# The opening of a four-image attention kernel on one core: x in four pieces, projections reordered, and the first weights' low parts made by GpSimd

## The chip, the core and the metric

The kernel runs on one core of a Trainium2 chip. The metric is the device time of one execution in microseconds (us), median of three runs. TensorE is the matmul engine (PE in the rows, PEld its weight loads), VectorE is DVE, ScalarE is ACT, GpSimd is POOL; SyncE (SP) only issues DMAs here. The engines run their instruction lists in order and wait for each other by semaphores.

## The reference

For each of four images `x` of 256 channels by 1024 pixels:

```python
q = einsum('oc,bcn->bon', Wq, xf) + bq        # 32 x 1024
k = einsum('oc,bcn->bon', Wk, xf) + bk        # 32 x 1024
v = einsum('oc,bcn->bon', Wv, xf) + bv        # 256 x 1024
scores = einsum('bqi,bqj->bij', q, k)         # 1024 x 1024
attn = softmax(scores, axis=-1)
out = einsum('bcj,bij->bci', v, attn) + x
```

## The kernel before

Every fp32 operand of a matmul is split in two: a high part, rounded to the matmul's type by a copy (a *cut*), and a low part, the difference (a *split*, a subtraction). A product is then high by high, low by high and high by low. A cut is a copy on ScalarE, VectorE or GpSimd; a split is a subtraction on VectorE or GpSimd.

Channels lie on partitions in two tiles (`CT` = 2). The work on one image has these stages:

- Projection of q and k (`qk_home`), q and k biased, cut, split and stacked into `q_a` and `k_a`, so that one matmul of 96 rows gives all three products. For image 0 `q_a` is filled in parts `Q_PARTS`: two quarters and the second half (called q2, cut and split by GpSimd in `split_q2`).
- Scores of pixel tile t (128 pixels by 1024) in PSUM, `first_scores(t)` for image 0. VectorE takes the negated maximum per row (`row_max`), ScalarE the sum of exponentials (`sum_exp`), which together are the shift of the softmax. VectorE turns the shifts into rows of `q_b`.
- v, projected in eight tiles (`v_tile`), two to a half bank, cut (`first_cut_v`) and split (`split_v`).
- Transposed scores (`scores_t(n)`, 128 by 512) with the shift in the matmul, exponentials by ScalarE (`exp(n)`: `w_full`, and for some n also the high part `w_hi`), the low part `w_lo` by VectorE or GpSimd (`split_w(n)`), and the weighting (`weigh_v`): four matmuls with `w_hi` and two with `w_lo`, the low products. There are 16 such tiles n per image.

Which engine makes `w_lo` of tile n is a table, `split_by_pool(n)`. In the steady state a table `FRONT` puts the projection and scores of the next image between the weighting steps of this one. Everything before the first weighting is written out by hand on each engine and is the opening; the first weighting step, `first_weigh_v`, is the last of it.

In the opening SyncE loads x of image 0 as two transfers of 512 KB, one for each channel tile, and then `wv`; ScalarE issues the transfer of `small_sb` (the weights of q and k, and the biases). ScalarE cuts x in four pieces of 512 columns, `piece(i)`; VectorE makes their low parts; TensorE runs three matmuls for each piece. Until then TensorE multiplies zeros (`keep_busy`). GpSimd copies `wqk_pair` (used from image 1 on), splits `wv`, copies the q quarters to their second place (`put_q_dup`), does `split_q2`, and then cuts and splits image 1's x in four quarters (`cut_x1`, `split_x1`), with `split_w(1)` and `split_w(3)` behind them. `shift_ready` stands for VectorE's shifts of the first four tiles; GpSimd's third quarter waits for it. `v_split` counts VectorE's splits of v.

Of the kernel before, what the change touches and what calls it, by code (L numbers as in the profile page):

```python
# [6 lines left out]
def nonlocal_attention(nc, x, small, wv_t, out):  # L7
# [6 lines left out]
    P = 128  # L14
# [24 lines left out]
    def split_by_pool(n):  # L39
        return n % PER in ((1, 3, 8, 9, 11, 13) if n < PER else (0, 8, 9, 11, 13))  # L40
# [19 lines left out]
    with ctx:  # L60
# [51 lines left out]
        x0_in = [sem(f"x0_in{c}") for c in range(CT)]  # L112
# [80 lines left out]
        def piece(i):  # L193

            return i // 2, cols(i % 2)
# [80 lines left out]
        def _(sp):  # L276
            for c in range(CT):
                sp.dma_start(x_sb[:, 0, c, :], x_v[0, :, c, :]).then_inc(x0_in[c], DMA)
# [82 lines left out]
        def _(pool):  # L361
# [52 lines left out]


# [6 lines left out]
            pool.wait_ge(pair_made, 2)  # L422
            pool.wait_ge(wv_cut, 1)
# [3 lines left out]
            put_q_dup(0)  # L427
            pool.wait_ge(q_dup_put, 1)
            put_q_dup(1)
            pool.wait_ge(q_dup_put, 2)  # L430
# [12 lines left out]
            pool.wait_ge(x1_split, 3)  # L443
            cut_x1(3)
            pool.wait_ge(x1_cut, 4)

            split_w(1)
# [36 lines left out]
        def _(act):  # L484
            act.dma_start(small_sb[:, :], small).then_inc(small_in, DMA)
            act.preload_act_table_set("natural_log_exp_and_others")
            for i in range(4):
                c, part = piece(i)
                act.wait_ge(x0_in[c], DMA)
                nc.scalar.activation(x_hi[:, 0, c, part], x_sb[:, 0, c, part], ACT.Copy).then_inc(x0_cut, 1)  # L490
# [66 lines left out]
            def put_q_hi():  # L557

                act.wait_ge(q_lo_put, 1)
                nc.scalar.activation(q_a[2 * CQK:3 * CQK, Q_PARTS[1]], q_home(1),  # L560
                                     ACT.Identity, bias=bias[2 * CQK:3 * CQK, 0:1]).then_inc(q_hi_put, 1)
# [17 lines left out]
            exp(0)  # L579
# [33 lines left out]
        def _(dve):  # L613
# [5 lines left out]
            def twice(w):  # L619
# [5 lines left out]
            dve.wait_ge(wqk_cut, 1)  # L625
            nc.vector.tensor_tensor(twice(wqk_lo), wqk, twice(wqk_hi).bitcast(fp32),
                                    ALU.subtract).then_inc(wqk_split, 1)

            for i in range(4):
                c, part = piece(i)  # L630
                dve.wait_ge(x0_cut, i + 1)
# [119 lines left out]
            def finish(b, h, c):  # L751
# [9 lines left out]
                if (b, h) == (0, 0):  # L761
# [84 lines left out]
        def _(pe):  # L846
# [23 lines left out]
            def first_project_qk(i):  # L870
                c, part = piece(i)
                dst = qk_home(0, i % 2)
                if i == 0:
                    pe.wait_ge(wqk_cut, 1)
                pe.wait_ge(x0_cut, i + 1)
                nc.tensor.matmul(dst, wqk_hi[:, c, :], x_hi[:, 0, c, part], start=(c == 0), stop=False)
                if i == 0:
                    pe.wait_ge(wqk_split, 1)
                nc.tensor.matmul(dst, wqk_lo[:, c, :], x_hi[:, 0, c, part], start=False, stop=False)
                pe.wait_ge(x0_split, i + 1)  # L880
                last = nc.tensor.matmul(dst, wqk_hi[:, c, :], x_lo[:, 0, c, part], start=False, stop=(c == CT - 1))  # L881
                if c == CT - 1:
                    last.then_inc(qk_ready, 1)
# [55 lines left out]
            def v_tile(b, t):  # L939
# [4 lines left out]
                if b == 0 and t == 0:  # L944

                    for c in range(CT):
                        for xs in (x_hi, x_lo):
                            nc.tensor.matmul(dst, xs[:, 0, c, px], wv_hi[:, c, :],
                                             start=(c == 0 and xs is x_hi), stop=False)
                    pe.wait_ge(wv_split, 1)  # L950
                    for c in range(CT):
                        nc.tensor.matmul(dst, x_hi[:, 0, c, px], wv_lo[:, c, :], start=False, stop=(c == CT - 1))
                    return
                last = group(dst, terms)
                if t % VT == VT - 1:
                    last.then_inc(v_ready, 1)

# [75 lines left out]
            def first_weigh_v():  # L1033
# [57 lines left out]
            v_tile(0, 3)  # L1091
            first_scores(3)
# [10 lines left out]
            def turn(b):  # L1103
                for s in range(PER):
# [15 lines left out]
                    if what == S:  # L1120
                        if b + image:
                            scores(b + image, k)
                        else:
# [40 lines left out]
```

## Time and profile before

| what | us |
|---|---|
| median of three runs | 164.04 (163.82 to 164.06) |
| the profiled execution | 163.81 |
| its span in the trace | 162.0 |
| TensorE busy | 157.5 |
| VectorE busy | 133.9 |
| ScalarE busy | 109.2 |
| GpSimd busy | 60.0 |

The span is what the trace covers, from the first instruction of the program to the last; the execution's own time has 1.8 us around it. A busy share is an average over stages: the opening, some 19 us, has other limits than the rest. In timeline rows the first number is the start in us from the span's beginning and the second the time busy; with "x4" the row merges four instructions and the time is that from the first's start to the last's end.

### The profile page before, as it was taken

Reading aid. Unit: us, or ns where it says so; the run is one execution under the profiler, and the core shown is the slowest. Engines: PE = TensorE matmul, PEld = TensorE weight load, DVE = VectorE, ACT = ScalarE, POOL = GpSimd, SP = SyncE. Lnnn points to the kernel's source line nnn. Section 1 sums busy time; section 2 is a strip of 40 time slices with the busy share of each in tenths; the row PEclk is TensorE's granted clock in tenths of the full one; section 3 lists DMA queues with packets and bytes.
Section 4 is the critical chain, followed back from the end, with each engine's and each line's share of the span. In section 5 each row is a group of like instructions: output and inputs, shape, how many; then the busy total and the mean of one; then the engine's idle time right before and its main releaser. Section 6 shows DMA issues by size and latency. Waiting matters only on the chain.

```text
span 162.0 us, 2456 instructions
## 1 busy us (share of the span) xinstructions
PE 157.5 (97%) x788; PEld 132.3 (82%) x788; DVE 133.9 (83%) x215; ACT 109.2 (67%) x200; POOL 60.0 (37%) x68
## 2 busy tenths in 40 slices
PE   7999999999999999999999999999999999999993
PEld 5677887798888887798888897788888898888882
DVE  1899998888988989997989989895989779846952
ACT  3679887969999545827999646736896655756400
POOL 4479946256222316348443300342333300124500
PEclk9999999999999999999999999999999999999999
DMA  4576672152103030162711130162320330003003
GB/s 161 187 299 166 243 235 89 31 151 63 55 0 97 1 129 2 37 144 67 268 39 49 54 129 0 37 146 67 121 61 1 97 129 0 0 5 129 0 0 130
DMA packets 7780, 14.67 MB, mean 91 GB/s; under 512 B 1504, under 2 KB 2072, under 8 KB 7768
## 3 DMA queue, kind: packets, MB, share of 16 engines
q1 hardware_dynamic: 6728, 13.46, 25.4%
q0 software_dynamic: 608, 0.80, 2.2%
q10 hardware_dynamic: 432, 0.26, 0.5%
q8 instruction: 6, 0.10, 0.3%
q14 instruction: 6, 0.05, 0.1%
HBM read 4.79 MB, written 4.20 MB: 55 GB/s over the span
## 4 chain that ended last, share of the span: by engine, by line
PE 90%; DMA 2%; ACT 2%; DVE 2%; issue 1%; DVEq 0%
PE acc L1009 32%; PE acc L1015 16%; PE slot L849 11%; PE st L996 9%; PE slot L909 7%; PE slot L1009 5%; DMA small_sb<-small 2%; PE slot L1015 2%; ACT dump L504 2%; PE slot L861 2%; PE slot L866 2%; PE slot L935 1%; DVE negmax L667 1%; PE slot L881 1%; DVE x_lo L632 0%
## 5 line engine op out<-in xcount | busy, mean ns | idle before, releaser
L402 POOL TENSOR_TENSOR w_lo<-w_full,w_hi 128x512 fp32r<-128x512 f32 x21 | 28.0, 1338 | 46.6 <-ACT w_full L542 25.4
L1009 PE MATMUL acc<-w_hi,v_hi 128*128 128x512 f32 x112 | 44.3, 395 | 0.0
L1009 PE MATMUL acc<-w_hi,v_lo 128*128 128x512 f32 x112 | 44.1, 394 | 0.0
L542 ACT ACTIVATE w_full<-st 128x512 f32<-128x512 f32 x62 | 36.8, 594 | 7.6 <-PE st L996 7.5
L504 ACT ACTIVATE dump<-slot,negmax 128x1024 f32<-128x1024 f32 x29 | 32.5, 1119 | 10.5 <-DVE negmax L667 10.1
L667 DVE TENSOR_REDUCE negmax<-slot 128x1 f32<-128x1024 f32 x29 | 35.2, 1217 | 2.7 <-PE slot L909 2.7
L1015 PE MATMUL acc<-w_lo,v_hi 128*128 128x512 f32 x112 | 37.4, 396 | 0.0
L734 DVE TENSOR_TENSOR w_lo<-w_full,w_hi 128x512 fp32r<-128x512 f32 x43 | 30.7, 719 | 3.6 <-issue 0.5
L1009 PEld LDWEIGHTS acc<-w_hi,v_hi 128*128 128x128 f32 x112 | 21.1, 189 | 5.0 <-issue 0.2
L1009 PEld LDWEIGHTS acc<-w_hi,v_lo 128*128 128x128 f32 x112 | 21.2, 189 | 4.8
L1015 PEld LDWEIGHTS acc<-w_lo,v_hi 128*128 128x128 f32 x112 | 21.0, 188 | 4.8
L996 PE MATMUL st<-q_b,k_b 98*128 98x512 f32 x62 | 24.5, 398 | 0.1
L725 DVE CAST w_hi<-w_full 128x512 fp32r<-128x512 f32 x40 | 19.5, 489 | 3.0 <-ACT w_full L542 1.5
L539 ACT ACTIVATE w_hi<-st 128x512 fp32r<-128x512 f32 x24 | 14.3, 594 | 6.2 <-PE st L996 6.0
L849 PE MATMUL slot<-wv_hi,x_hi 128*128 128x256 f32 x62 | 17.4, 281 | 0.4 <-ACT dump L504 0.4
L849 PE MATMUL slot<-wv_lo,x_hi 128*128 128x256 f32 x62 | 17.4, 281 | 0.0
L849 PE MATMUL slot<-wv_hi,x_lo 128*128 128x256 f32 x62 | 17.3, 280 | 0.0
L909 PE MATMUL slot<-k_a,q_a 96*128 96x512 f32 x48 | 15.2, 397 | 0.0
L531 ACT ACTIVATE v_hi<-slot 128x512 fp32r<-128x512 f32 x12 | 7.2, 599 | 11.8 <-PE slot L849 11.8
L265 POOL DMA_DIRECT2D q_b<-shift_rows x7 | 4.2, 602 | 29.5 <-DVE shift_rows L706 27.0
L715 DVE TENSOR_TENSOR v_lo<-slot,v_hi 128x512 fp32r<-128x512 f32 x16 | 11.0, 690 | 3.8 <-ACT v_hi L531 3.7
L909 PEld LDWEIGHTS slot<-k_a,q_a 96*128 96x128 f32 x48 | 13.0, 310 | 1.1
(102 smaller groups left out, 225.2 us busy)
## 6 DMA issues: line engine op xcount, KB each, us to landing
out<-x_sb SPq DMA_DIRECT2D x7, 512.0 KB, 2.8
x_sb<-x SPq DMA_DIRECT2D x3, 1024.0 KB, 5.1
k_b<-k_a SPq DMA_DIRECT2D x8, 192.0 KB, 2.6
q_b<-q_a SPq DMA_DIRECT2D x8, 192.0 KB, 2.6
x_sb<-x SPq DMA_DIRECT2D x2, 512.0 KB, 4.2
k_a<-qk_parts SPq DMA_DIRECT2D x12, 64.0 KB, 2.0
q_a<-qk_parts SPq DMA_DIRECT2D x12, 64.0 KB, 2.2
k_a<-qk_parts POOLq DMA_DIRECT2D x6, 64.0 KB, 2.2
```

The lines of the kernel that those rows point to most:

```text
L402: nc.gpsimd.tensor_tensor(w_lo[:, r, :], w_full[:, r, :], w_hi[:, r, :].bitcast(fp32), ALU.subtract).then_inc(w_split_pool, 1)
L504: nc.scalar.activation(dump[:, t % 2, :], s_home(b, t), ACT.Exp, bias=negmax[:, t:t + 1], accum_out=rowsum[:, t:t + 1]).then_inc(rowsum_re ...
L539: nc.scalar.activation(w_hi[:, r, :], st_home(n), ACT.Exp).then_inc(w_cut_act, 1)
L542: nc.scalar.activation(w_full[:, r, :], st_home(n), ACT.Exp).then_inc(exp_done, 1)
L667: nc.vector.tensor_reduce(out=negmax[:, t:t + 1], in_=s_home(b, t), op=ALU.max, axis=AX.X, negate=True).then_inc(negmax_ready, 1)
L725: nc.vector.tensor_copy(w_hi[:, r, :], w_full[:, r, :]).then_inc(w_cut_dve, 1)
L734: nc.vector.tensor_tensor(w_lo[:, r, :], w_full[:, r, :], w_hi[:, r, :].bitcast(fp32), ALU.subtract).then_inc(w_split_dve, 1)
L849: last = nc.tensor.matmul(dst, lhs, rhs, start=(i == 0), stop=(i == len(terms) - 1))
L909: last = nc.tensor.matmul(s_home(b, t)[:, cols(h)], pixels(b, t), k_a[0:K_A, cols(h)], start=True, stop=True)
L996: nc.tensor.matmul(st_home(n), k_b[0:K_B, j * P:(j + 1) * P], q_b[0:K_B, cols(h)], start=True, stop=True).then_inc(st_ready, 1)
L1009: nc.tensor.matmul(dst, v[:, b % 2, j, c * P:(c + 1) * P], w_hi[:, n % RING, part], start=(j == 0 and v is v_hi), stop=False)
L1015: return nc.tensor.matmul(dst, v_hi[:, b % 2, j, c * P:(c + 1) * P], w_lo[:, n % RING, part], start=False, stop=(j == JT - 1))
```

## The change

The table gives tile 0's low part to GpSimd, which makes it just before that of tile 1 and ahead of its cut of x1's last quarter. On TensorE the low products of tile 0 come behind the scores of tile 5, the sixth tile, and not behind those of tile 4. Besides:

- x of image 0 comes in four transfers of 256 KB, each with its semaphore, in the order of the halves (both channel tiles of the first 512 pixels, then the second). The small transfer is issued by SyncE behind the first.
- The projection of q and k is ordered by halves, so the first half is through before the second.
- ScalarE makes the high part of q's first quarter (VectorE did) and cuts `wv` only behind the high parts of q and k. Its first cut of v stands behind the sums.
- GpSimd copies q's first quarter ahead of `wqk_pair` and the second behind it, then splits `wv`.
- TensorE's high products for v tile 0 stand behind tile 0's scores, its low ones and v tile 1 behind the scores of tile 2; tile 3's scores stand before v tile 3.
- VectorE splits k before q, and v's second pair of tiles before the first.

```diff
-        return n % PER in ((1, 3, 8, 9, 11, 13) if n < PER else (0, 8, 9, 11, 13))
+        return n % PER in ((0, 1, 3, 8, 9, 11, 13) if n < PER else (0, 8, 9, 11, 13))
...
-            return i // 2, cols(i % 2)
+            return i % CT, cols(i // CT)
...
-            for c in range(CT):
-                sp.dma_start(x_sb[:, 0, c, :], x_v[0, :, c, :]).then_inc(x0_in[c], DMA)
+            for i in range(4):
+                c, part = piece(i)
+                sp.dma_start(x_sb[:, 0, c, part], x_v[0, :, c, part]).then_inc(x0_in[i], DMA)
+                if i == 0:
+                    sp.dma_start(small_sb[:, :], small).then_inc(small_in, DMA)
...
+            put_q_dup(0)
+            pool.wait_ge(q_dup_put, 1)
...
             pool.wait_ge(pair_made, 2)
+            put_q_dup(1)
+            pool.wait_ge(q_dup_put, 2)
             pool.wait_ge(wv_cut, 1)
...
-            put_q_dup(0)
-            pool.wait_ge(q_dup_put, 1)
-            put_q_dup(1)
-            pool.wait_ge(q_dup_put, 2)
...
             pool.wait_ge(x1_split, 3)
+            split_w(0)
+            split_w(1)
             cut_x1(3)
             pool.wait_ge(x1_cut, 4)
 
-            split_w(1)
...
-            act.dma_start(small_sb[:, :], small).then_inc(small_in, DMA)
...
+            act.wait_ge(small_in, DMA)
+            put_k_hi(0)
+            put_q_hi(0)
+            put_k_hi(1)
+            put_q_hi(1)
             act.wait_ge(wv_in, DMA)
             nc.scalar.activation(wv_hi[:, :, :], wv[:, :, :], ACT.Copy).then_inc(wv_cut, 1)
-            act.wait_ge(small_in, DMA)
-            put_k_hi(0)
-            put_k_hi(1)
-            put_q_hi()
             put_q2_full()
-            first_cut_v(0)
             for t in range(TH):
                 sum_exp(0, t)
             put_first_rows()
+            first_cut_v(0)
...
-            dve.wait_ge(qk_ready, 1)
-            nc.vector.tensor_scalar(out=q_a[2 * CQK:3 * CQK, Q_PARTS[0]], in0=q_home(0),
-                                    scalar1=bias[2 * CQK:3 * CQK, 0:1], scalar2=None,
-                                    op0=ALU.add).then_inc(q_hi_put, 1)
+            put_k_lo(0)
             put_q_lo(0)
-            put_k_lo(0)
...
             first_shifts()
-            split_v(0, 0)
             first_cut_v(1)
             split_v(0, 1)
+            first_cut_v(2)
+            split_v(0, 0)
             invert_sums()
-            first_cut_v(2)
             split_v(0, 2)
...
                 if h == 0 and j % VT == 0:
-                    pe.wait_ge(v_split, 4 * b + 1 + j // VT)
+
+                    pe.wait_ge(v_split, 4 * b + 1 + j // VT if b + j else 2)
...
                 first_scores(TH)
+                scores_t(AHEAD)
+
+                first_scores(TH + 1)
                 for c in range(CT):
                     last = weigh_low(0, 0, 0, c, acc[:, c, :], slice(0, HALF))
                 last.then_inc(av_done, 1)
-                scores_t(AHEAD)
...
-            keep_busy(20, QUARTER)
-            for i in range(4):
-                first_project_qk(i)
-            pe.wait_ge(wv_cut, 1)
-            v_tile(0, 0)
-            v_tile(0, 1)
+            keep_busy(16, QUARTER)
+            first_project_all()
+
+            keep_busy(4, QUARTER)
             first_scores(0)
+            first_v_high()
             first_scores(1)
             first_scores(2)
+            first_v_low()
+            v_tile(0, 1)
 
             pe.wait_ge(q2_full_put, 1)
             v_tile(0, 2)
+            first_scores(3)
             v_tile(0, 3)
-            first_scores(3)
```

On GpSimd, from the copy of the weight pair to q2, this stood before:

```order
L418 CAST wqk_pair<-wqk_hi 128x2x64 [waits wqk_cut,ones_put]
L418 CAST wqk_pair<-wqk_lo 128x2x64 [waits wqk_split]
L424 TENSOR_TENSOR wv_lo<-wv,wv_hi 128x512 [waits wv_cut,pair_made]
L374 CAST q_a<-q_a 32x256 [waits q_hi_put,wv_split]
L374 CAST q_a<-q_a 32x256 [waits q_hi_put,q_dup_put]
L380 CAST q_a<-qk_rest 32x512 [waits q2_full_put,q_dup_put]
```

and now:

```order
L377 CAST q_a<-q_a 32x256 [waits q_hi_put,ones_put]
L423 CAST wqk_pair<-wqk_hi 128x2x64 [waits wqk_cut,q_dup_put]
L423 CAST wqk_pair<-wqk_lo 128x2x64 [waits wqk_split]
L377 CAST q_a<-q_a 32x256 [waits q_hi_put,pair_made]
L431 TENSOR_TENSOR wv_lo<-wv,wv_hi 128x512 [waits wv_cut,q_dup_put]
L383 CAST q_a<-qk_rest 32x512 [waits q2_full_put,wv_split]
```

The two copies of q have moved ahead of the split of `wv`, one of them ahead of the pair; `wv_lo` is now the last before q2.

On GpSimd, from the third quarter of image 1's x on, before:

```order
L408 CAST x_hi<-x_sb 128x2x256 [waits shift_ready,x1_split]
L412 TENSOR_TENSOR x_lo<-x_sb,x_hi 128x2x256 [waits x1_cut]
L408 CAST x_hi<-x_sb 128x2x256 [waits x1_split]
L402 TENSOR_TENSOR w_lo<-w_full,w_hi 128x512 [waits w_cut_act,exp_done,x1_cut]
L402 TENSOR_TENSOR w_lo<-w_full,w_hi 128x512 [waits w_cut_act,exp_done,w_split_dve]
```

and now:

```order
L411 CAST x_hi<-x_sb 128x2x256 [waits shift_ready,x1_split]
L415 TENSOR_TENSOR x_lo<-x_sb,x_hi 128x2x256 [waits x1_cut]
L405 TENSOR_TENSOR w_lo<-w_full,w_hi 128x512 [waits w_cut_act,exp_done,x1_split]
L405 TENSOR_TENSOR w_lo<-w_full,w_hi 128x512 [waits w_cut_act,exp_done]
L411 CAST x_hi<-x_sb 128x2x256
```

The low parts of weights 0 and 1 stand directly behind the third quarter, and the cut of the last quarter behind both.

On TensorE, at the end of the opening (`acc<-w_hi` is the weighting with high weights, `acc<-w_lo` the low products, `slot<-k_a` scores, `st<-q_b` transposed scores), before:

```order
L1009 MATMUL acc<-w_hi,v_lo 128x512
L935 MATMUL slot1<-k_a,q_a 128x512 [waits v_split,q2_lo_put,q2_dup_put]
L935 MATMUL slot1<-k_a,q_a 128x512
L1015 MATMUL acc<-w_lo,v_hi 128x512 [waits w_split_dve] x2
L996 MATMUL st<-q_b,k_b 128x512 [waits exp_done]
L935 MATMUL slot0<-k_a,q_a 128x512 [waits v_split]
L935 MATMUL slot0<-k_a,q_a 128x512
```

and now:

```order
L1026 MATMUL acc<-w_hi,v_lo 128x512
L948 MATMUL slot1<-k_a,q_a 128x512 [waits v_split,q2_lo_put,q2_dup_put]
L948 MATMUL slot1<-k_a,q_a 128x512
L1012 MATMUL st<-q_b,k_b 128x512 [waits exp_done]
L948 MATMUL slot0<-k_a,q_a 128x512 [waits v_split]
L948 MATMUL slot0<-k_a,q_a 128x512
L1032 MATMUL acc<-w_lo,v_hi 128x512 [waits w_split_pool] x2
```

The low products have moved behind three matmuls, and wait for GpSimd instead of VectorE.

## Rows read from the trace of the kernel before

**Rows 1.** The page's chain that ended last: shares of the span by engine.

```profile
PE 90%; DMA 2%; ACT 2%; DVE 2%; issue 1%; DVEq 0%
```

**Rows 2.** Busy time by stretch: length, PE, PEld, DVE, ACT, POOL, clock, DMA, GB/s.

```profile
4.50:5.00 0.50, 0.50 (x4) 0.38 (x3) 0.29 (x1) 0.50 (x1) 0.00 (x0) 1.00 0.97 401
...
40.00:80.00 40.00, 40.00 (x197) 33.95 (x197) 36.44 (x58) 29.29 (x55) 16.27 (x16) 1.00 0.26 79
```

**Rows 3.** The chain in order of time: start, us, what.

```profile
0.75 3.94 DMA small_sb<-small
...
18.42 0.71 PE slot L849 x6
```

**Rows 4.** DMAs: x's time from issue to landing, and the small weights'.

```profile
DMA to landing us min/median/max: 3.7/4.6/4.8
...
small_sb<-small ACTq DMA_DIRECT2D x1, 66.0 KB, 3.9
```

**Rows 5.** Timeline of the projection: start, us, engine, line, operation.

```profile
4.50 1.15 ACT L490 ACTIVATE x_hi<-x_sb 128x512 fp32r<-128x512 f32 x2 [2.04 <-DMA x_sb<-x]
...
5.04 0.43 DVE L626 TENSOR_TENSOR wqk_lo<-small_sb,wqk_hi 128x256 fp32r<-128x256 f32 x1
...
5.27 0.59 PE L876 MATMUL slot<-x_hi,wqk_hi 128*128 128x512 f32 x1
5.38 2.68 DVE L632 TENSOR_TENSOR x_lo<-x_sb,x_hi 128x512 fp32r<-128x512 f32 x4
...
5.70 0.40 PE L879 MATMUL slot<-x_hi,wqk_lo 128*128 128x512 f32 x1
...
8.41 0.39 PE L881 MATMUL slot<-x_lo,wqk_hi 128*128 128x512 f32 x1
```

**Rows 6.** Timeline behind it: wv, k and q, and the first maximum.

```profile
6.88 0.62 ACT L569 ACTIVATE wv_hi<-wv 128x512 fp32r<-128x512 f32 x1
...
8.21 1.31 ACT L554 ACTIVATE k_a<-slot,small_sb 64x512 fp32r<-64x512 f32 x2 [0.72 <-PE slot L881]
...
9.18 1.40 DVE L642 SCALAR_TENSOR_TENSOR k_a<-slot,small_sb,k_a 32x512 fp32r<-32x512 f32 x2
...
9.55 0.47 ACT L560 ACTIVATE q_a<-slot,small_sb 32x256 fp32r<-32x256 f32 x1
...
11.17 1.23 DVE L667 TENSOR_REDUCE negmax<-acc 128x1 f32<-128x1024 f32 x1
```

**Rows 7.** Timeline of GpSimd, VectorE's split of weights 0, and GpSimd's w_lo (ns).

```profile
5.14 0.47 POOL L418 CAST wqk_pair<-wqk_hi 128x128 fp32r<-128x128 f32 x1 [2.30 <-DVE wqk_hi L624]
...
5.56 0.75 POOL L418 CAST wqk_pair<-wqk_lo 128x128 fp32r<-128x128 f32 x1
...
7.64 1.58 POOL L424 TENSOR_TENSOR wv_lo<-wv,wv_hi 128x512 fp32r<-128x512 f32 x1 [1.34 <-ACT wv_hi L569]
...
10.72 0.61 POOL L380 CAST q_a<-qk_rest 32x512 fp32r<-32x512 f32 x1 [0.18 <-ACT qk_rest L565]
...
19.53 0.68 DVE L734 TENSOR_TENSOR w_lo<-w_full,w_hi 128x512 fp32r<-128x512 f32 x1
19.59 1.10 POOL L408 CAST x_hi<-x_sb 128x512 fp32r<-128x512 f32 x1
...
L402 POOL TENSOR_TENSOR w_lo<-w_full,w_hi x21: 1283/1297/1721, 20.9 to 152.4; 128x512 fp32r<-128x512 f32 x21
```

**Rows 8.** Timeline of TensorE at the first weighting steps.

```profile
18.97 0.47 PE L1009 MATMUL acc<-w_hi,v_hi 128*128 128x512 f32 x1
...
21.63 0.39 PE L996 MATMUL st<-q_b,k_b 98*128 98x512 f32 x1
...
23.25 0.84 PE L935 MATMUL slot<-k_a,q_a 96*128 96x512 f32 x2
...
23.93 0.39 PE L996 MATMUL st<-q_b,k_b 98*128 98x512 f32 x1
```

**Rows 9.** The page's costliest groups: VectorE's split of v, mean ns.

```profile
L715 DVE TENSOR_TENSOR v_lo<-slot,v_hi 128x512 fp32r<-128x512 f32 x16 | 11.0, 690 | 3.8 <-ACT v_hi L531 3.7
```

More of the change, by code:

```diff
@@ L110, in nonlocal_attention @@
         slot = [ctx.enter_context(nc.psum_tensor(f"slot{i}", [P, N], fp32)) for i in range(2)]
-        x0_in = [sem(f"x0_in{c}") for c in range(CT)]
+        x0_in = [sem(f"x0_in{i}") for i in range(4)]
         x1_in = sem("x1_in")
@@ L488, in _ @@
                 c, part = piece(i)
-                act.wait_ge(x0_in[c], DMA)
+                act.wait_ge(x0_in[i], DMA)
                 nc.scalar.activation(x_hi[:, 0, c, part], x_sb[:, 0, c, part], ACT.Copy).then_inc(x0_cut, 1)
@@ L555, in put_k_hi, with put_q_hi @@
                                      ACT.Identity, bias=bias[0:2 * CQK, 0:1]).then_inc(k_hi_put, 1)
-            def put_q_hi():
-                act.wait_ge(q_lo_put, 1)
-                nc.scalar.activation(q_a[2 * CQK:3 * CQK, Q_PARTS[1]], q_home(1),
+            def put_q_hi(i):
+                if i:
+                    act.wait_ge(q_lo_put, i)
+                nc.scalar.activation(q_a[2 * CQK:3 * CQK, Q_PARTS[i]], q_home(i),
                                      ACT.Identity, bias=bias[2 * CQK:3 * CQK, 0:1]).then_inc(q_hi_put, 1)
@@ L624, in _ @@
             nc.vector.tensor_copy(twice(wqk_hi), wqk).then_inc(wqk_cut, 1)
-            dve.wait_ge(wqk_cut, 1)
-            nc.vector.tensor_tensor(twice(wqk_lo), wqk, twice(wqk_hi).bitcast(fp32),
-                                    ALU.subtract).then_inc(wqk_split, 1)
             for i in range(4):
                 c, part = piece(i)
+                if i == 1:
+                    dve.wait_ge(wqk_cut, 1)
+                    nc.vector.tensor_tensor(twice(wqk_lo), wqk, twice(wqk_hi).bitcast(fp32),
+                                            ALU.subtract).then_inc(wqk_split, 1)
                 dve.wait_ge(x0_cut, i + 1)
@@ L868, in project_qk, with first_project_qk, first_project_all @@
                 both_halves(CT - 1).then_inc(qk_ready, 1)
-            def first_project_qk(i):
+            def first_project_qk(i, w, xs):
                 c, part = piece(i)
[L872 to L883, printed above, removed]
+                return nc.tensor.matmul(qk_home(0, i // CT), w[:, c, :], xs[:, 0, c, part],
+                                        start=(c == 0 and w is wqk_hi and xs is x_hi),
+                                        stop=(c == CT - 1 and xs is x_lo))
+            def first_project_all():
+                pe.wait_ge(wqk_cut, 1)
+                pe.wait_ge(x0_cut, 1)
+                first_project_qk(0, wqk_hi, x_hi)
+                pe.wait_ge(x0_split, 1)
+                first_project_qk(0, wqk_hi, x_lo)
+                pe.wait_ge(x0_cut, 2)
+                first_project_qk(1, wqk_hi, x_hi)
+                pe.wait_ge(wqk_split, 1)
+                first_project_qk(0, wqk_lo, x_hi)
+                first_project_qk(1, wqk_lo, x_hi)
+                pe.wait_ge(x0_split, 2)
+                first_project_qk(1, wqk_hi, x_lo).then_inc(qk_ready, 1)
+                for i in (2, 3):
+                    pe.wait_ge(x0_cut, i + 1)
+                    first_project_qk(i, wqk_hi, x_hi)
+                    first_project_qk(i, wqk_lo, x_hi)
+                    pe.wait_ge(x0_split, i + 1)
+                    last = first_project_qk(i, wqk_hi, x_lo)
+                last.then_inc(qk_ready, 1)
             def pixels(b, t):
@@ L943, in v_tile @@
                          for xs, w in ((x_hi, wv_hi), (x_hi, wv_lo), (x_lo, wv_hi))]
[L944 to L953, printed above, removed]
                 last = group(dst, terms)
@@ L956, in v_tile, with first_v_high, first_v_low @@
                     last.then_inc(v_ready, 1)
+            def first_v_high():
+                pe.wait_ge(wv_cut, 1)
+                for c in range(CT):
+                    for xs in (x_hi, x_lo):
+                        nc.tensor.matmul(v_home(0, 0)[:, 0:C], xs[:, 0, c, 0:P], wv_hi[:, c, :],
+                                         start=(c == 0 and xs is x_hi), stop=False)
+            def first_v_low():
+                pe.wait_ge(wv_split, 1)
+                for c in range(CT):
+                    nc.tensor.matmul(v_home(0, 0)[:, 0:C], x_hi[:, 0, c, 0:P], wv_lo[:, c, :],
+                                     start=False, stop=(c == CT - 1))
             def project_v(b, g):
@@ L1122, in turn @@
                             scores(b + image, k)
-                        else:
+                        elif s:
                             first_scores(k)
```

## The prediction

> **What bounds the kernel now.** I read the chain of waits first. It lies on TensorE for 90% of the span, and its largest lines are the products with v [rows 1]. Then I read the busy time by stretch: from 40 to 80 us TensorE is busy 40.00 us of 40 [rows 2]. From the first weighting at 18.97 us on, matmuls follow each other at 0.23 us per 512 columns, with one hole that counts: the scores of tile 6, at 23.25, take 0.84 us for two, and the next matmul is at 23.93 where 23.25 + 0.46 would be 23.71: 0.22 late [rows 8]. The change leaves TensorE's later work alone, so only the opening can move the time. The question is when TensorE is through the low products of the first weights and whether it runs without a hole from there. In the opening the chain starts with a DMA, 3.94 us for the small weights [rows 3].
>
> **Landings.** The two 512 KB halves of x land 3.7 and about 4.6 us after their issues at 0.74 and 1.2, so at 4.45 and 5.8; the small weights at 4.66 [rows 4]. At 401 GB/s [rows 2] 256 KB take 0.65 us. With pieces of 256 KB I estimate the first at 4.45 - 0.65 = 3.8, the small weights behind it at 4.0 (66 KB, 0.17 us), the next pieces at 4.65, 5.3 and 5.95. No row shows a first piece of this size; bounds are 3.45 (another 256 KB less in flight in the slow beginning) and 4.3 (as slow as the whole half, nearly). I take 3.8.
>
> **Projection of q and k.** ScalarE cuts piece 0 in 0.61 us, to 4.45. VectorE then does four x_lo (2.68 us) and wqk_lo (0.36 from start to start) from 4.5 to 7.55; the second x_lo ends at 6.25 [rows 5]. The matmul behind it ends near 6.7, where the first half had been ready at 8.11; the last of twelve starts at 7.7 and ends at 8.1, against 8.80 [rows 5]. From here by the rows' durations [rows 6]: ScalarE k_hi(0) 6.8 to 7.5, q_hi(0) to 7.95, k_hi(1) 8.2 to 8.9, VectorE k_lo(0) 7.55 to 8.3, q_lo(0) to 8.8, then ScalarE q_hi(1) 8.85 to 9.3, wv_hi 9.25 to 9.85, q2_full to 10.5; VectorE k_lo(1) 8.95 to 9.7, q_lo(1) to 10.15. The first maximum starts at 10.2 instead of 11.17: 0.97 us earlier.
>
> **TensorE until the first weights.** Behind tile 0's scores come four matmuls, the scores of 1 and 2, the low products of v (wv_lo at 11.25, below), and two v tiles of 0.71 each [rows 3], so tile 3's scores are through at 13.7, where VectorE, three maxima of 1.13 behind 10.2, would be free at 13.6: 0.1 of the 0.97 is lost there. The fourth maximum, the shifts, the sum, the rows and v tiles 6 and 7 are the same operations in the same order as before and keep 0.87. VectorE has to give two splits of v before the weighting may start (one before), and the order cut, split, cut, split at 0.7 each [rows 9] behind the shifts (before near 16.3, then 15.4) has them at 18.1 to 18.2, the same. The weighting starts at 18.1 instead of 18.97 [rows 8].
>
> **GpSimd.** Here the gain goes. The copy of q (0) waits for q_hi(0), 8.0 to 8.4. The two copies of the weight pair stand behind it now. They took 0.47 and 0.75 beside VectorE's subtractions; alone I take 0.32 each, to 9.1 (bounds: 0.61 for four times the elements in the same kind of copy says it could be 0.2, the two rows say 0.47 and 0.75). Copy (1) 9.35 to 9.75. wv_lo waits for wv_hi, 9.9, and ran 1.58 us while VectorE's x_lo reached 0.42 us into it, to 8.06 [rows 5, 7]; the same form on w_lo takes 1.297 median, 1.283 to 1.721 [rows 7]. I take 1.29, to 11.25, for VectorE then has only work from PSUM. q2 starts at 11.3, before 10.72 [rows 7]. From q2's first copy to the end of the third x_lo of image 1 the order is unchanged: 19.59 - 10.72 = 8.87 us without a gap over 0.2 [rows 7]. So the subtraction of weights 0, which VectorE did at 19.53 [rows 7], starts at 20.2, ends at 21.5, and TensorE can use it at 21.55.
>
> TensorE comes to those low products at 18.1 + 0.93 (four high) + 0.47 (scores 4) + 0.23 (transposed 2) + 0.47 (scores 5) = 20.2. It stands for 1.35 us. Queued behind the waiting matmul are transposed scores 3, the weighting with tile 1 and all that follows, and ScalarE's exponentials wait for these. The two low products end at 22.0. Before, the same set of work was done at 21.63, where transposed scores 3 start [rows 8]: 0.39 us late. Weights 1 follow on GpSimd at once, 21.5 to 22.8; TensorE wants them at 22.0 + 0.23 + 0.93 = 23.2, in time. Scores 6 then start at 23.65, their sum condition long met, so the hole of 0.22 goes. Sum: +0.39 - 0.22 = **+0.17 us**.
>
> What costs nothing: the copy of a quarter of x1 put behind the weights would be due 3 us later. VectorE loses 0.6 us of subtraction and gains a slack that nobody waits for. The four extra idle matmuls (16 + 4 in place of 20) fill 0.47 us of the wait for k_lo. The last transposed scores, issues on SP and DMAs of k_b and q_b come earlier or have over 3 us.
>
> A row on the common path: the copy of x1's last quarter took 1.10 us at 19.59, where its three sisters took 0.61, and VectorE was subtracting w_lo from 19.53 to 20.21 [rows 7]. The Trainium skill (SBUF — State Buffer, Who interferes with whom) says that a VectorE instruction with two SBUF inputs and a GpSimd one that reads SBUF lock each other out, the second waiting until the first is through; the trace agrees. By that rule VectorE's two small shift operations near 15.2 would also wait for GpSimd's x_lo, up to 0.7 us, and VectorE's cut of weights 2, near 22.1, until 22.8. In my sum neither counts: the weighting would start at 18.8 rather than 18.1, inside the 1.35 us of standing, and weights 2 are wanted at 24.1. By the rule the sum would stay +0.17.
>
> **The profiled execution** took 163.81, so 163.98 after; the median of the three runs is 0.23 above it, which gives 164.2 for the measured time.
>
> **Rivals.**
> *GpSimd is in time or nearly (faster).* If pieces land at the early bound and hand-offs cost less than in my steps, q2 starts at 10.7, as it did before, weights 0 are ready at 20.95 and the two low products end at 21.4: 0.23 ahead, with the hole another 0.22, 0.45 in all: 163.6. For it: 3.45 is not excluded. Against it: 0.6 us must be found in six hand-offs that the rows price. If GpSimd did not bind at all, 1.35 more than the forecast could be won, 162.9, which I hold for out of reach.
> *GpSimd's chain is longer (slower).* It decides from the point where q2 starts after 11.45. wv_lo at 1.58 again adds 0.29, the pair copies at 0.47 and 0.75 push copy (1) and add 0.1, a first landing at 4.1 adds 0.2: +0.6 and so 164.8. For it: all three prices stand in rows.
> *TensorE runs the projection at half rate (slower).* The first two real matmuls start 0.43 us apart (5.27 to 5.70) [rows 5], later ones 0.23. Those 0.43 for 512 columns are the 1.2 GHz level, although the granted clock reads 1.00 there [rows 2]. In the changed order it has holes around 5, at 8.5 and of 0.7 us before k_lo(1). If the rise comes only after the projection, eleven matmuls cost 0.20 more each, 2.2 us, of which 0.3 lie in waits for x_lo: q and k are ready near 10.0, 1.9 later, and all of it goes through GpSimd's chain: 166.1. The Trainium skill (TensorE: Matmul & The Clock Gate, What's actually happening) says that activity releases the clock and idleness takes it back, which speaks for this rival; that the clock rose within the projection in this trace speaks against it.
> *The change does not do what it says*: the first piece lands at 4.45 as the whole half did. Then GpSimd's chain is 0.65 longer, 164.9; I count this with the second rival.
>
> **Chances.** Forecast (own range 163.8 to 164.6) 0.62; GpSimd in time 0.14; longer chain 0.16; half rate 0.08. A measurement of this kernel can tell about 0.2%, 0.33 us, from no change. Of the forecast's 0.62 some 0.04 lies below 163.71 and 0.16 above 164.37. So faster 0.18, same 0.42, slower 0.40. The range goes down just past the faster rival, to 163.5, and up past the longer chain, to 165.0; the half-rate case is left out.
>
> **What would show it.** Right: q and k's first half ready near 6.7, the first maximum near 10.2, the weighting from 18.1 to 18.8, GpSimd without a gap from wv_lo at 9.9 to the end of weights 1, and a hole of about a microsecond before TensorE's first low products, put down to GpSimd's w_lo; from 24 us on TensorE as before, some 0.2 later. Wrong: if that hole is under 0.5 us, if GpSimd's w_lo starts before 19.6, if matmuls after 5.3 stand 0.43 apart, or if TensorE shows holes behind 24 us.

## The result, and the profile after

| | before | after |
|---|---|---|
| median, us | 163.96 (163.80 to 164.20, 6 runs) | 165.63 (165.05 to 166.06, 6 runs) |
| profiled execution, us | 163.81 | 165.60 |
| its span, us | 162.0 | 163.8 |

The ratio is 1.0099, interval 1.0075 to 1.0123: the change makes the kernel 1.67 us slower. 164.2 was forecast (163.98 for the profiled execution), and 165.0 was the top of the range.

The chain of waits of after still lies on TensorE, but a DMA of x has taken the place of the small weights' [rows 1, 3]:

```profile
PE 88%; ACT 3%; DMA 3%; POOL 1%; DVE 1%; SPq 1%; issue 0%; DVEq 0%; POOLq 0%
```

The same chain in order of time (start, us, what) leads from the third piece of x, issued at 2.12 and landed at 6.80, over q and k, the last maximum and ScalarE's sums to GpSimd's chain:

```profile
2.12 4.68 DMA x_sb<-x
7.51 1.94 PE slot L873 x6
...
15.20 1.24 DVE negmax L672
16.46 1.21 ACT dump L507 x2
20.55 1.06 POOL x_lo L415
21.69 1.29 POOL w_lo L405
```

The beginning of after's timeline (start, us, engine, line, operation) answers to rows 5:

```profile
0.74 0.38 SPq L279 DMA_DIRECT2D x_sb<-x  x1
1.19 0.42 SPq L281 DMA_DIRECT2D small_sb<-small  x1
1.65 1.38 SPq L279 DMA_DIRECT2D x_sb<-x  x3
3.07 0.43 SPq L282 DMA_DIRECT2D wv<-wv_t  x1
3.60 0.63 ACT L493 ACTIVATE x_hi<-x_sb 128x512 fp32r<-128x512 f32 x1 [1.57 <-DMA x_sb<-x]
3.78 0.29 DVE L629 CAST wqk_hi<-small_sb 128x256 fp32r<-128x256 f32 x1 [2.50 <-DMA small_sb<-small]
...
5.42 0.63 ACT L493 ACTIVATE x_hi<-x_sb 128x512 fp32r<-128x512 f32 x1 [1.18 <-DMA x_sb<-x]
...
6.82 1.23 ACT L493 ACTIVATE x_hi<-x_sb 128x512 fp32r<-128x512 f32 x2 [0.78 <-DMA x_sb<-x]
...
7.96 0.66 ACT L557 ACTIVATE k_a<-slot,small_sb 64x512 fp32r<-64x512 f32 x1
```

The first piece and the small weights land as forecast (3.6 and 3.8). The second piece lands at 5.4 instead of 4.65, the last two at 6.8 instead of 5.3 and 5.95, and ScalarE, which takes its list in order, can make k's high part only at 7.96, when it has cut both. Busy time by stretch (length, PE, PEld, DVE, ACT, POOL, clock, DMA share, GB/s) says how the queue went; first after:

```profile
3.00:4.00 1.00, 1.00 (x6) 0.69 (x5) 0.22 (x1) 0.40 (x1) 0.00 (x0) 1.00 0.79 202
4.00:5.00 1.00, 0.84 (x5) 0.33 (x2) 0.81 (x3) 0.23 (x1) 0.00 (x0) 1.00 0.81 250
5.00:6.00 1.00, 0.51 (x1) 0.19 (x1) 0.29 (x1) 0.58 (x1) 0.00 (x0) 1.00 0.89 311
```

then before, in the first two of the same stretches:

```profile
3.00:4.00 1.00, 1.00 (x6) 0.71 (x5) 0.00 (x0) 0.00 (x0) 0.00 (x0) 1.00 1.06 410
4.00:5.00 1.00, 1.00 (x7) 0.73 (x5) 0.29 (x1) 0.50 (x1) 0.00 (x0) 1.00 0.99 408
```

In these two stretches after's DMA engines are busy for 79 and 81% of the time and move 49 and 61% of the bytes. The rest of after's opening in the timeline (answers to rows 6 to 8):

```profile
11.52 1.22 DVE L672 TENSOR_REDUCE negmax<-acc 128x1 f32<-128x1024 f32 x1
...
12.80 0.60 POOL L383 CAST q_a<-qk_rest 32x512 fp32r<-32x512 f32 x1
...
16.19 1.29 POOL L415 TENSOR_TENSOR x_lo<-x_sb,x_hi 128x512 fp32r<-128x512 f32 x1
...
16.53 0.97 DVE L679 CAST shift_parts<-negmax 128x4 fp32r<-128x4 f32 x1
...
20.28 0.50 PE L1026 MATMUL acc<-w_hi,v_hi 128*128 128x512 f32 x1
...
21.69 2.52 POOL L405 TENSOR_TENSOR w_lo<-w_full,w_hi 128x512 fp32r<-128x512 f32 x2
...
23.02 0.73 PE L1032 MATMUL acc<-w_lo,v_hi 128*128 128x512 f32 x2 [0.36 <-POOL w_lo L405]
23.59 0.40 PE L1012 MATMUL st<-q_b,k_b 98*128 98x512 f32 x1
...
25.70 0.39 PE L1012 MATMUL st<-q_b,k_b 98*128 98x512 f32 x1
```

The first maximum comes at 11.52 (before 11.17), q2 on GpSimd at 12.80 (10.72), the weighting at 20.28 (18.97), transposed scores 3 at 23.59 (21.63) and 4 at 25.70 (23.93): 1.77 us late, and from there on the difference stays at that to the end. All of it is lost in the opening.

### The profile page after: what moved, and what is told of

Same layout as the page of the kernel before. It is cut to its first block, busy times and chain, and to the rows that moved or that the text cites. A ratio compares the mean times of both kernels' runs of the same rounds, so it can differ in the third digit from the quotient of the medians.

```text
span 163.8 us, 2459 instructions
## 1 busy us (share of the span) xinstructions
PE 157.5 (96%) x788; PEld 131.5 (80%) x788; DVE 134.1 (82%) x213; ACT 110.1 (67%) x201; POOL 59.7 (36%) x69
## 4 chain that ended last, share of the span: by engine, by line
PE 88%; ACT 3%; DMA 3%; POOL 1%; DVE 1%; SPq 1%; issue 0%; DVEq 0%; POOLq 0%
PE acc L1026 31%; PE acc L1032 16%; PE slot L850 11%; PE st L1012 8%; PE slot L922 7%; PE slot L1026 5%; DMA x_sb<-x 3%; PE slot L1032 2%; PE slot L862 2%; PE slot L867 2%; PE slot L873 1%; PE slot L948 1%; POOL w_lo L405 1%; DVE negmax L672 1%; ACT dump L507 1%; POOL x_lo L415 1%
## 5 line engine op out<-in xcount | busy, mean ns | idle before, releaser
L405 POOL TENSOR_TENSOR w_lo<-w_full,w_hi 128x512 fp32r<-128x512 f32 x22 | 29.3, 1334 | 46.0 <-ACT w_full L545 25.2
L739 DVE TENSOR_TENSOR w_lo<-w_full,w_hi 128x512 fp32r<-128x512 f32 x42 | 30.0, 719 | 3.3
L1026 PEld LDWEIGHTS acc<-w_hi,v_lo 128*128 128x128 f32 x112 | 21.2, 189 | 4.8
```

The costliest lines, as they stand in the source:

```text
L405: nc.gpsimd.tensor_tensor(w_lo[:, r, :], w_full[:, r, :], w_hi[:, r, :].bitcast(fp32), ALU.subtract).then_inc(w_split_pool, 1)
L739: nc.vector.tensor_tensor(w_lo[:, r, :], w_full[:, r, :], w_hi[:, r, :].bitcast(fp32), ALU.subtract).then_inc(w_split_dve, 1)
L1026: nc.tensor.matmul(dst, v[:, b % 2, j, c * P:(c + 1) * P], w_hi[:, n % RING, part], start=(j == 0 and v is v_hi), stop=False)
```

## The experiments

Each run's time is compared with runs of the kernel before on the same chip (medians 163.82 to 163.88). Two questions were put: what made the opening late, and what the named part of the change costs (weights 0 subtracted by GpSimd, the low products behind the sixth tile's scores). Trace rows are of one execution per kernel, and a number in brackets behind another is that of the kernel before.

### The small transfer back on ScalarE

```diff
                 sp.dma_start(x_sb[:, 0, c, part], x_v[0, :, c, part]).then_inc(x0_in[i], DMA)
-                if i == 0:
-                    sp.dma_start(small_sb[:, :], small).then_inc(small_in, DMA)
...
+            act.dma_start(small_sb[:, :], small).then_inc(small_in, DMA)
             act.preload_act_table_set("natural_log_exp_and_others")
```

> The changed kernel with one thing put back: the small weights' transfer is issued by ScalarE on its own queue, not by SyncE between x's first two pieces. Theory A (pieces of 256 KB in 2 KB rows on one queue move slowly by themselves, 190 to 300 GB/s where 4 KB rows moved at 400): the last pieces still land near 6.8 us, the small weights at 4.6 and not 3.75, the time stays at 165.3 to 166.0. Theory B (the small transfer's short rows inside SyncE's queue slow the pieces behind it): piece 2 lands near 4.7 instead of 5.4, the last near 6.0 instead of 6.8, and the time falls by about 0.8 us, to 164.8.

Measured: 164.69 us, ratio 1.0050 (1.0034 to 1.0067), 0.94 us less than after. Its timeline:

```profile
0.74 1.80 SPq L279 DMA_DIRECT2D x_sb<-x  x4
...
4.77 1.34 ACT L492 ACTIVATE x_hi<-x_sb 128x512 fp32r<-128x512 f32 x2 [0.36 <-DMA x_sb<-x]
...
6.38 0.63 ACT L492 ACTIVATE x_hi<-x_sb 128x512 fp32r<-128x512 f32 x1 [0.27 <-DMA x_sb<-x]
...
11.67 0.60 POOL L381 CAST q_a<-qk_rest 32x512 fp32r<-32x512 f32 x1
...
15.42 0.95 DVE L678 CAST shift_parts<-negmax 128x4 fp32r<-128x4 f32 x1
...
20.56 2.53 POOL L403 TENSOR_TENSOR w_lo<-w_full,w_hi 128x512 fp32r<-128x512 f32 x2
...
21.89 0.74 PE L1031 MATMUL acc<-w_lo,v_hi 128*128 128x512 f32 x2 [0.36 <-POOL w_lo L403]
```

The second piece is in at 4.77, the last at 6.38, and everything behind is 1.1 us earlier. The four issues on SyncE stand 0.46 us apart; with the small one among them the later pieces are issued that much later too. So the place of the 66 KB transfer costs some 0.9 us. What is left, 0.8 us over before, has another cause. The third piece shows the cost best: its cut started at 6.82 in after and 6.94 in after_no_gps (below), which has the same transfers; in small_by_act it is done by 6.11. The second piece varies by itself: it was cut at 5.42 in after, but at 4.73 in after_no_gps.

### Two transfers, four transfers, two queues

*two_transfers*: after with the small one on ScalarE and x in two transfers of 512 KB.

```diff
-            for i in range(4):
-                c, part = piece(i)
-                sp.dma_start(x_sb[:, 0, c, part], x_v[0, :, c, part]).then_inc(x0_in[i], DMA)
+            for c in range(CT):
+                sp.dma_start(x_sb[:, 0, c, :], x_v[0, :, c, :]).then_inc(x0_in[c], DMA)
...
```

> The changed kernel with x in two transfers of 512 KB as before and the small weights issued by ScalarE; the order of all arithmetic stays changed. Theory A and B both put x's halves at 4.45 and 5.8 us again. The projection by halves is then through for the first half near 7.6 (changed: 7.9) and for the second near 9.0 (changed: 9.4), so 0.4 us earlier than in the changed kernel: 165.2. Theory C (the transfers do not matter, the order of the work behind them does): no change, 165.6.

Measured: 165.30 us, ratio 1.0119 (1.0082 to 1.0157); the interval is wide, since two of its six runs were near 167. The first maximum is at 11.22, q2 at 12.50: 0.3 us earlier than in after, as is the time.

*before_four*: the reverse edit in the kernel before, whose piece order (by channel tiles) stays.

> The kernel before with one thing changed: x comes in four transfers of 256 KB on SyncE's queue, in the old order (both halves of channel tile 0, then of tile 1), the small weights still on ScalarE's queue. Theory A: the last piece lands 0.8 to 1.0 us later than the second half did (6.7 instead of 5.8), and the time rises to about 164.8. Theory B: it lands at 5.8 or 5.9 and the time stays at 164.0.

Measured: 163.81 us, ratio 0.9995 (0.9980 to 1.0010), single runs from 163.24 to 164.53. Four pieces in one queue cost nothing here, as theory B had it, but gain nothing either. The first maximum is at 10.71 (11.17), and q2 at 10.11 (10.72). In the profiled execution (164.35, one of the longer of its twelve) the gain is lost at the shifts, where two rows of its timeline stand over each other:

```profile
15.54 1.27 POOL L413 TENSOR_TENSOR x_lo<-x_sb,x_hi 128x512 fp32r<-128x512 f32 x1
...
15.64 1.18 DVE L677 TENSOR_TENSOR shift_parts<-negmax,shift_parts 128x4 fp32r<-128x4 f32 x1
```

An operation on 4 elements per partition, 0.17 us where it is alone, ends when GpSimd's subtraction does. This wait of one engine for the other is called the lock below.

*two_queues*: after with the named part undone, the small transfer and pieces 1 and 3 issued by ScalarE.

> As the kernel with both things put back (small weights on ScalarE's queue, VectorE subtracting for weights 0), with x's pieces 1 and 3 issued by ScalarE behind the small weights and pieces 0 and 2 by SyncE. Theory H (what limits the pieces is the one queue that carries them): the pieces land 0.3 to 0.6 us sooner, the last at 5.7, and the time is 163.6. Theory I (the total rate near 400 GB/s limits them): the last at 6.2 to 6.4 as on one queue, ScalarE's issues of 0.4 us each cost nothing before 3.6 us, and the time is that of the kernel on one queue.

Measured: 165.18 us, ratio 1.0093 (1.0066 to 1.0121). The first maximum is at 10.86, later than with one queue in the kernel that it is to be compared with (small_by_act_no_gps, below: 10.65 and 165.03). The second queue bought nothing here.

### The named part alone, and taken away

*headline_on_before*: the kernel before with only the named part.

```diff
-        return n % PER in ((1, 3, 8, 9, 11, 13) if n < PER else (0, 8, 9, 11, 13))
+        return n % PER in ((0, 1, 3, 8, 9, 11, 13) if n < PER else (0, 8, 9, 11, 13))
...
+            split_w(0)
+            split_w(1)
             cut_x1(3)
...
                 first_scores(TH)
+                scores_t(AHEAD)
+                first_scores(TH + 1)
                 for c in range(CT):
                     last = weigh_low(0, 0, 0, c, acc[:, c, :], slice(0, HALF))
                 last.then_inc(av_done, 1)
-                scores_t(AHEAD)
...
-                        else:
+                        elif s:
                             first_scores(k)
```

The last lines keep the sixth tile's scores, now issued in the opening, from being issued a second time.

> The kernel before with the named part of the change alone: GpSimd subtracts for weights 0 and 1 ahead of its cut of x1's last quarter, and TensorE's low products of weights 0 stand behind the scores of the sixth tile. Theory D (GpSimd's subtraction is what the time is lost on): GpSimd's queue is at this point at 19.59, gives weights 0 at 20.9, and TensorE arrives at 21.1, so even here it has no slack; if anything is late, a hole of some tenths and 164.2. Theory E (the loss comes from the opening before it; here the subtraction is in time): no hole, VectorE is free 0.6 us earlier and takes the fifth tile's maximum at 20.6, and the hole of 0.22 us before tile 6's scores goes: 163.75.

Measured: 164.40 us, ratio 1.0029 (1.0018 to 1.0040): slower. But not in the opening: the low products start at 21.37, 0.14 behind the matmul before them, and transposed scores 4 start at 23.95 (23.93). The loss is at 42 us, on VectorE:

```profile
42.31 0.69 DVE L735 TENSOR_TENSOR w_lo<-w_full,w_hi 128x512 fp32r<-128x512 f32 x1 [0.50 <-issue]
42.92 1.22 DVE L668 TENSOR_REDUCE negmax<-slot 128x1 f32<-128x1024 f32 x1
44.05 1.56 DVE L638 TENSOR_TENSOR x_lo<-x_sb,x_hi 128x512 fp32r<-128x512 f32 x1
```

VectorE stands for 0.50 us for nothing that the profile shows ("issue"). That puts its subtraction behind GpSimd's `w_lo` of 43.77, which it then has to sit out (1.56 instead of 0.68); from 52 us on TensorE is 0.67 later. The kernel before has one such stall as well, elsewhere. Its `w_lo` there is followed at once by the next operation (102.47):

```profile
101.75 0.69 DVE L734 TENSOR_TENSOR w_lo<-w_full,w_hi 128x512 fp32r<-128x512 f32 x1 [0.46 <-issue]
```

*gps_with_filler*: the same kernel with an instruction put on VectorE where the moved subtraction had stood, so that its list keeps its length.

```diff
+            nc.vector.memset(filler[:, :], 0.0)
             split_v(0, 3)
...
```

> The named part of the change alone on the kernel before, as in the run that took 164.40, with one addition: a memset of 128 by 8 on VectorE, whose result nobody reads, where its subtraction for weights 0 stood, so that its list has as many instructions as before. In the 164.40 run the two traces agreed within 0.02 us until 42 us; there VectorE stood 0.50 us before a subtraction for no wait that the profile shows (in the kernel before such a stand of 0.46 is at 101.75), GpSimd's w_lo got in ahead of VectorE's x_lo, which then took 1.56 us instead of 0.68, and TensorE lost 0.67 us by 52 us. Theory F (the stand belongs to a place in VectorE's instruction list): with the filler it goes back to near 101.8 and the time is 163.9. Theory G (the shifted timing of the opening brings it about): still 164.4.

Measured: 163.50 us, ratio 0.9980 (0.9971 to 0.9988): 0.9 us less than without the memset. The stall at 42 us is gone, and none is seen near 101.75 either, where theory F had put it:

```profile
41.77 0.69 DVE L736 TENSOR_TENSOR w_lo<-w_full,w_hi 128x512 fp32r<-128x512 f32 x1
...
102.29 0.16 DVE L690 TENSOR_TENSOR shift<-negmax,logsum 128x4 f32<-128x4 f32 x1 [0.39 <-ACT logsum L511]
```

At 102.29 VectorE waits 0.39 us for ScalarE. A stall there could hide in this wait, and in before it can hardly have cost time, for the same operation started only 0.18 later behind it. With the memset the kernel is 0.3 us faster than before: TensorE is 0.09 ahead of it at 24 us, 0.17 at 79 and 0.26 at 110. What the memset does alone, in the kernel before, was not tried, so the 0.3 us are not shown to be the named part's.

The stall goes with VectorE's list rather than with the time: before_four and four_unlocked (below), which have before's list, show it at the same instruction, at 102.28 and at 101.40. What it is, and whether it is a fixed place in the list, stays open. After shows no such stall, with or without the named part.

*after_no_gps* and *small_by_act_no_gps*: the named part undone in after, and in small_by_act.

> The changed kernel without its named part: VectorE subtracts for weights 0 again, GpSimd cuts x1's last quarter ahead of weights 1, and the low products stand behind the fifth tile's scores as before. Theory A (GpSimd's late subtraction costs what the changed trace shows: low products at 23.02 where TensorE arrives at 22.5, transposed scores 3 at 23.59): VectorE would have weights 0 at 21.5, transposed scores 3 start near 22.9 and the time falls by 0.5 to 0.7 us, to 165.0. Theory B (the loss is all in the transfers and the shifts ahead of it, and the hole only takes over from another wait, such as GpSimd's weights 1 behind the cut, due at 24.1): 165.4 to 165.6.

> The changed kernel with two things put back: the small weights' transfer on ScalarE's queue, and the named part undone (VectorE subtracts for weights 0, low products behind the fifth tile's scores). What is left is the order of x's pieces and the reordered opening. The kernel with the first of the two alone took 164.69 and had the weighting at 19.15, before 18.97, and transposed scores 3 at 22.47, before 21.63. Theory A: without GpSimd's subtraction these start near 21.8, and the time is 164.0, the kernel before's. Theory B (other waits take over): 164.4 or more.

Measured: 165.67 us, ratio 1.0110 (1.0082 to 1.0139), against 165.63 with the named part; and 165.03, ratio 1.0085 (1.0053 to 1.0118), against 164.69 with it. In both VectorE's own subtraction of weights 0 is held by GpSimd, as in this row of small_by_act_no_gps:

```profile
19.95 1.35 DVE L737 TENSOR_TENSOR w_lo<-w_full,w_hi 128x512 fp32r<-128x512 f32 x1
```

By these medians the named part cost nothing in after: without it other waits take its place, VectorE's held subtraction and the hole at scores 6.

### GpSimd's subtractions kept off VectorE's shifts

*small_by_act_unlocked* (and the same in *small_by_act_no_gps_unlocked*):

```diff
             cut_x1(0)
-            split_x1(0)
-            pool.wait_ge(x1_split, 1)
             cut_x1(1)
+            pool.wait_ge(shift_ready, 1)
+            split_x1(0)
             split_x1(1)
             pool.wait_ge(x1_split, 2)
-            pool.wait_ge(shift_ready, 1)
```

> The kernel after with the small transfer issued by ScalarE as before, and on GpSimd the cuts of image 1's first two quarters, then the wait for VectorE's shifts, then the two subtractions: no GpSimd subtraction stands over VectorE's two shift operations. The run with the small transfer put back alone took 164.69 (ratio 1.0050). Theory L (the lock sets the opening): the shift cut takes 0.2 us instead of 0.95, the weighting starts near 18.5 instead of 19.15, and the time falls by 0.5 to 0.65, to 164.1. Theory G (GpSimd's chain sets the opening, the lock is covered by it): the cut takes 0.2 and the weighting is early as well, but w_lo of tile 0 on GpSimd still starts at 20.5 to 20.7, the hole ahead of TensorE's first low products grows from 0.36 to about 1.0 us, and the time stays at 164.6 to 164.9.

Measured: 164.60 us, ratio 1.0043 (1.0031 to 1.0055), against 164.69. The shift cut is free, and the time is the same:

```profile
6.34 0.90 PE L871 MATMUL slot<-x_hi,wqk_lo 128*128 128x512 f32 x2
...
12.23 0.61 POOL L381 CAST q_a<-qk_rest 32x512 fp32r<-32x512 f32 x1
...
15.97 0.17 DVE L677 CAST shift_parts<-negmax 128x4 fp32r<-128x4 f32 x1
...
21.10 2.52 POOL L403 TENSOR_TENSOR w_lo<-w_full,w_hi 128x512 fp32r<-128x512 f32 x2
...
22.42 0.73 PE L1030 MATMUL acc<-w_lo,v_hi 128*128 128x512 f32 x2 [0.91 <-POOL w_lo L403]
```

The time is theory G's. The hole at the low products has grown from 0.36 to 0.91 us, but not by an earlier weighting, as theory G had it. In this profiled execution (164.98, the longest of its six) everything ahead of the shifts was later: q2 came at 12.23 rather than 11.67, although the pieces were cut at nearly the same times (4.71 and 6.54). TensorE's matmuls before 7 us stand 0.43 apart, where small_by_act had 0.23 from 5.7 on:

```profile
5.94 0.63 PE L872 MATMUL slot<-x_hi,wqk_lo 128*128 128x512 f32 x2
```

So the weighting is at 19.11, as early as with the lock, and not at 18.5, while GpSimd's subtraction starts 0.54 later. From q2 to that subtraction are 8.87 us again; the wait for the shifts, 0.33 us of idle, did not lengthen it.

> The same edit of GpSimd's order, in the kernel in which VectorE makes the low part of weights 0 again and the low products stand where they stood before (165.03, ratio 1.0085 with the lock). Here nothing of GpSimd stands ahead of the first low products. If the lock sets the opening: the shift cut takes 0.2 us, the weighting starts near 18.8 instead of 19.43, and the time falls by 0.5 to 0.7, to about 164.4. If weights 1 on GpSimd or VectorE's subtraction of weights 0 (which a GpSimd subtraction can hold as well) come next: it falls by less than 0.3.

Measured: 164.53 us, ratio 1.0036 (1.0023 to 1.0049), against 165.03: 0.5 us less. Where nothing of GpSimd stands ahead of the first low products, keeping its subtractions off VectorE does gain time: at the shifts, and at VectorE's own subtraction of weights 0, which takes 0.68 us here for 1.35. What each gave is not told apart. The next hole is 0.45 us, for GpSimd's weights 1.

*four_filler_unlocked*: gps_with_filler with x in four transfers, the small one on ScalarE, and `pool.wait_ge(shift_ready, 1)` moved from ahead of `cut_x1(2)` to ahead of `split_x1(1)`. *four_unlocked*: before_four with the wait moved in the same way.

> The kernel before with GpSimd's subtraction of weights 0, the late low products and the memset of 128x8 on VectorE (163.50, ratio 0.998), and x of image 0 in four transfers of 256 KB, the small one on ScalarE, and GpSimd's wait for the shifts moved ahead of its second subtraction of x. Theory G (GpSimd's chain from q2 on sets the first low products): q2 starts at 10.1, 0.6 earlier, the idle for the shifts takes 0.4 back, weights 0 are ready at 21.0 to 21.2 and TensorE wants them near 20.3 to 20.5: a hole of 0.5 to 0.8 us and a time of 163.2 to 163.5. Without such a hole (weights in time) 162.9 would be reached.

Measured: 163.15 us, ratio 0.9959 (0.9945 to 0.9973), the fastest of all: 0.7 us under before and 2.5 under after. Its rows:

```profile
10.09 0.61 POOL L382 CAST q_a<-qk_rest 32x512 fp32r<-32x512 f32 x1 [0.18 <-ACT qk_rest L568]
...
15.27 0.19 DVE L677 CAST shift_parts<-negmax 128x4 fp32r<-128x4 f32 x1
...
19.16 2.53 POOL L404 TENSOR_TENSOR w_lo<-w_full,w_hi 128x512 fp32r<-128x512 f32 x2
...
20.66 0.63 PE L1019 MATMUL acc<-w_lo,v_hi 128*128 128x512 f32 x2
```

q2 starts 0.63 earlier than before, weights 0 are ready at 20.45, and TensorE comes to them with nearly no hole. I had put weights 0 at 21.0 to 21.2, half a microsecond too late, by bad adding: 10.1 for q2, the chain of 8.87, 0.3 of idle and 1.3 of subtraction make 20.6.

> The kernel before with x of image 0 in four transfers of 256 KB (163.81, ratio 0.9995, with VectorE's second shift operation at 1.18 us under GpSimd's subtraction), and GpSimd's wait for the shifts moved ahead of its second subtraction of x. If the lock took the gain of the pieces: the shift operation takes 0.17, the weighting starts near 18.4 instead of 19.29, and the time is 163.2 to 163.4, ratio near 0.997. If something else took it, it stays at 163.8.

Measured: 163.66 us, ratio 0.9988 (0.9977 to 0.9999). The shift operation takes 0.17 us and the weighting starts at 18.58 (before_four 19.29), so in these two executions the lock did hold that gain; but the median fell by 0.15 us where 0.4 to 0.6 was expected, and the two intervals overlap. Its last piece is cut at 6.33 and single runs lie from 163.30 to 164.08, so part of the rest is in how the pieces land. I can't give it a share.

## Why the prediction was wrong

- **What bounds the kernel, and no loss behind 24 us.** Right: the difference stands at transposed scores 4 (+1.77) and stays.
- **Landings.** The step that failed. The first piece (3.6 for 3.8) and the small weights (3.8 for 4.0) were right. I priced the small transfer at its 66 KB, 0.17 us, and let every later piece land at 401 GB/s; it had no effect on its neighbours in the sum. After shows 202 and 250 GB/s behind it, and the later pieces at 5.4 and 6.8 for 4.65, 5.3 and 5.95. The sum had no term either for an issue every 0.46 us on SyncE, although rows of before show 0.74 and 1.2. Putting that one transfer back gives 0.94 us of the time and 1.13 of the 1.50 us by which q2 came late. Whether its short rows or the later issues do it stays open.
- **Projection.** "k_hi(0) 6.8" was 7.96, since ScalarE cuts pieces 2 and 3 first and those landed last. wv_hi came at 10.67 (9.25), wv_lo at 11.45 (9.9), q2 at 12.80 (11.3).
- **GpSimd's chain.** Right, in mechanism and length: 8.87 us from q2 to weights 0 were forecast; 8.89 were measured in after, 8.89 in small_by_act, 8.87 with the wait moved. The time follows the start of q2: the profiled execution less that start is 165.60 - 12.80 = 152.80 in after, 164.45 - 11.67 = 152.78 in small_by_act, 165.30 - 12.50 = 152.80 in two_transfers and 164.98 - 12.23 = 152.75 in small_by_act_unlocked. The forecast's 163.98 less its 11.3 is 152.68. So of the 1.62 us that it missed in the profiled execution, 1.50 are the start of q2, and the sum behind q2 was right to 0.12.
- **The hole at the low products.** Forecast 1.35, measured 0.36, below the 0.5 that I had named as a sign against me. GpSimd did end last there; but TensorE also came late, with the weighting at 20.28 for 18.1. Of these 2.2 us some 1.3 stood already at the first maximum (11.52 for 10.2), and some 0.8 were the lock.
- **The lock.** I said that VectorE's shifts would wait up to 0.7 us for GpSimd and that it would cost nothing under the standing. In after the shift cut took 0.97 us for 0.20. The Trainium skill (SBUF — State Buffer, Who interferes with whom) names VectorE instructions with two SBUF inputs, and counts a cast among those that can take the ports shared with GpSimd too; the traces agree with both, 1.18 us for the two-input operation in before_four and 0.97 for the cast in after. That the lock was covered is shown by small_by_act_unlocked (164.60 against 164.69), and that the cover is the named part by small_by_act_no_gps_unlocked, where the same edit gave 0.5 us (at the shifts and at VectorE's own subtraction together).
- **The hole of 0.22 at scores 6.** It went, as forecast.
- **Rivals.** "GpSimd's chain is longer" named the right engine, with q2 far beyond the 11.45 from which it was to decide, but none of its three terms came in: `wv_lo` took 1.28 us and not 1.58, the copies of the pair 0.29 each, and the first piece was in at 3.6 and not 4.1. Its 164.8 would have been nearer by luck; the late pieces were in no rival. The half rate did not decide in after, whose matmuls stand 0.23 apart from 6.4 us on; in the profiled execution of small_by_act_unlocked it lasted until 7 us, and q2 was 0.56 later than in small_by_act.

What is left of small_by_act over before, 0.8 us, is by the same chain: its q2 starts 0.95 later than before. There the copies of q and the cut of `wv` come ahead of the split of `wv`, and that is the likely cause; the order was not tried by itself.

## What to carry to other kernels

Before a transfer is split or another is put between its pieces, count the issues in that queue and look at what each later piece does then: here a small transfer was not priced by its bytes. Follow the chain to the engine whose long run of work ends last, here GpSimd from q2 on, whose start alone gave the time to 0.1 us in four kernels; what happened beside it, the lock too, was covered. And where an instruction leaves an engine's list, look for an unexplained stall far behind.

## What the runs showed of the hardware

- A 66 KB transfer (528 bytes to each partition) in the queue behind the first of four of 256 KB (2 KB to each): from 3 to 4 and from 4 to 5 us 202 and 250 GB/s in after, and 273 and 231 in after_no_gps. With it in another queue: 338 and 272 in small_by_act, 315 and 260 in small_by_act_no_gps. With two transfers of 512 KB: 410 and 408 (before). How much of it is the short rows and how much the later issues isn't told apart.
- VectorE operations on 128x4 elements, of one input as well as of two, took 0.95 to 1.18 us beside a GpSimd subtraction (0.97 in after, 1.18 in before_four), and 0.17 to 0.20 alone (four_filler_unlocked, before).
- VectorE stands 0.46 to 0.50 us ("issue") once in some kernels: at 101.75 us in before, at 102.28 and 101.40 before the same instruction in before_four and four_unlocked, and at 42.31 with one instruction less (164.40 us); with the memset in its place none is seen (163.50). What happens there is open.
- With the granted clock at 1.00, matmuls of 512 columns stood 0.43 us apart until 6.8 us in one execution (small_by_act_unlocked) and 0.23 apart from 5.7 us in another with the same code on TensorE (small_by_act). What decides it was not tried.
